# A four-layer gated transformer on one core: second ternary rows rounded on ScalarE, ternary weights on VectorE, instruction lists given by a table

## The reference

```python
x = x + tanh(g_xattn[0]) * _L0_xattn_ref(ctx, ctx, _layernorm(x), ...)
x = x + tanh(g_ffn[0])   * _L0_ffn_ref(_layernorm(x), ...)        # butterfly, folded to two dense products
x = x + tanh(g_xattn[1]) * _L1_xattn_ref(_layernorm(x), ctx, ctx, mask, ...)
x = x + tanh(g_ffn[1])   * _L1_ffn_ref(_layernorm(x), ...)        # top-2 of 8 small experts
x = x + tanh(g_xattn[2]) * _L2_xattn_ref(_layernorm(x), ctx, ctx, ...)
x = x + tanh(g_ffn[2])   * _L2_ffn_ref(_layernorm(x), ...)        # ternary weights
x = x + tanh(g_xattn[3]) * _L3_xattn_ref(_layernorm(x), ctx, ctx, ..., mask)
x = x + tanh(g_ffn[3])   * _L3_ffn_ref(_layernorm(x), ...)        # top-2 of 8 gated experts
```

```python
def bitlinear(x, w, b):
    xn = x * rsqrt(mean(square(x)) + 1e-6)
    xq = clip(round(xn * s), -128, 127) / s        # s = 127 / max(max|xn|, 1e-5), per token
    wq = clip(round(w * t), -1, 1) / t             # t = 1 / max(mean|w|, 1e-5), of the whole matrix
    return einsum('bsi,oi->bso', xq, wq) + b
h = gelu(bitlinear(x, w1, b1))                     # 256 -> 1024
return bitlinear(h, w2, b2)                        # 1024 -> 256
```

## Time and profile before

| | us |
|---|---|
| median of 3 runs | 2720.06 (2715.66 to 2722.37) |
| the profiled execution | 2716.3 |
| its span, first to last instruction | 2714.5 |
| mean granted TensorE clock | 0.975 of full speed |

### The profile page before, as it was taken

How to read it: one execution, slowest core, us unless ns; L and a number is a source line. 1 busy time by engine, 2 the same in 40 slices (tenths; PEclk the granted TensorE clock), 3 DMA queues, 4 the chain that set the end, 5 groups by cost and what they waited for, 6 DMA issues and landing times.

```text
span 2714.5 us, 53760 instructions
## 1 busy us (share of the span) xinstructions
PE 2508.9 (92%) x21317; PEld 1693.2 (62%) x21317; DVE 1688.8 (62%) x4598; ACT 1041.0 (38%) x1654; POOL 976.1 (36%) x2413
## 2 busy tenths in 40 slices
PE   6999788999999988899999998889999998889999
PEld 4566444677767644577776754457776765446776
DVE  6545888755533588955543478885554358887542
ACT  4544345432234445523224444542322444453221
POOL 2352522444332332243442243233444323224342
PEclk8999889999999999999999999999999999899999
DMA  3200100000000000000000000000000000000000
GB/s 125 81 11 1 52 32 14 1 9 9 9 9 12 12 2 14 1 1 9 9 9 9 11 12 1 12 1 9 9 9 9 11 1 12 1 1 1 5 5 8
DMA packets 16280, 37.38 MB, mean 14 GB/s; under 512 B 1408, under 2 KB 11424, under 8 KB 15008
## 3 DMA queue, kind: packets, MB, share of 16 engines
q1 hardware_dynamic: 16032, 33.94, 3.5%
HBM read 29.74 MB, written 4.19 MB: 13 GB/s over the span
## 4 chain that ended last, share of the span: by engine, by line
PE 69%; DVE 22%; ACT 4%; issue 3%; POOL 2%; DMA 0%; SPq 0%; DVEq 0%; ACTq 0%; POOLq 0%
PE P L1322 8%; PE P L1134 4%; PE P L1142 4%; PE P L1181 4%; PE P L1355 4%; PE P L1323 4%; PE P L1193 4%; PE P L1340 4%; PE P L1114 4%; PE P L1331 4%; PE P L1035 4%; DVE mx L1721 4%; PE P L1206 3%; PE P L1031 2%; PE P L1044 1%
## 5 line engine op out<-in xcount | busy, mean ns | idle before, releaser
L1721 DVE TENSOR_REDUCE mx<-P 128x8 f32<-128x1232 f32 x256 | 369.0, 1441 | 178.1 <-PE P L1040 85.9
L1322 PE MATMUL P<-xT,w 128*128 128x256 f32 x1024 | 264.8, 381 | 0.7 <-DVE R L1956 0.3
L1477 ACT ACTIVATE ET<-P 128x2048 f32<-128x2048 f32 x96 | 180.2, 1877 | 162.4 <-PE P L1117 115.3
L1772 DVE SCALAR_TENSOR_TENSOR x<-P,w_first,x 128x512 f32<-128x512 f32 x96 | 73.9, 769 | 252.8 <-PE P L1181 87.0
L1322 PEld LDWEIGHTS P<-xT,w 128*128 128x128 f32 x1024 | 192.0, 190 | 60.7 <-issue 34.9
L792 POOL TENSOR_TENSOR sm<-sm 128x2 f32<-128x2 f32 x384 | 76.0, 198 | 421.0 <-DVE sm L1717 401.0
L1949 DVE SCALAR_TENSOR_TENSOR gu<-gu,P 128x256 f32<-128x256 f32 x128 | 53.9, 421 | 256.7 <-ACT gu L1528 256.7
L1035 PE MATMUL P<-KB,R 32*128 32x308 f32 x1536 | 162.0, 492 | 34.5 <-ACT ET L1477 14.7
L1528 ACT ACTIVATE gu<-P 128x256 f32<-128x256 f32 x128 | 49.2, 384 | 355.9 <-PE P L1323 334.4
L1114 PE MATMUL P<-R,KB 32*128 32x256 f32 x2048 | 169.6, 417 | 14.9 <-DVE mx L1721 14.8
L1434 ACT ACTIVATE xn<-x,sm 128x256 f32<-128x256 f32 x256 | 139.1, 592 | 100.9 <-POOL sm L800 100.9
(11 more groups left out here) (307 smaller groups left out, 5580.8 us busy)
## 6 DMA issues: line engine op xcount, KB each, us to landing
kvw<-in_wkv SPq DMA_DIRECT2D x12, 672.0 KB, 3.9
x<-in_x SPq DMA_DIRECT2D x16, 256.0 KB, 2.8
out<-x SPq DMA_DIRECT2D x16, 256.0 KB, 2.1
w<-in_w SPq DMA_DIRECT2D x2, 1024.0 KB, 5.9
w<-in_wexp SPq DMA_DIRECT2D x1, 1028.0 KB, 7.6
w_w<-in_wcon SPq DMA_DIRECT2D x1, 1024.0 KB, 9.9
w_w<-in_m3t SPq DMA_DIRECT2D x1, 1024.0 KB, 8.3
w<-in_w1q SPq DMA_DIRECT2D x1, 1024.0 KB, 10.3
```

What stands on the lines that cost most here:

```text
L1322: e.matmul(o, wm[:, c, js], s.xT[:, c, :], start=n == c == 0, stop=False, skip_group_check=True)
L1477: e.activation(ET[:].rearrange("p g c -> p (g c)"), quad.rearrange("p g c -> p (g c)"), ACT.Exp, bias=mb1[:, b:b + 1] if l == 1 else 0.0). ...
L1721: e.tensor_reduce(s.mx[:, i, :, 2 * u:2 * u + 2], quad[:, :, 0:2 * NK].rearrange("p g (a k) -> p g a k", a=2), AX.X, ALU.max).then_inc(q_d, 1)
```

## The change

It has five parts.

1. **Rounding.** A new stage `rd` on ScalarE does what L1910 and L1912 did on DVE, in two instructions over 128x1024, with the rounding constant and its negative as biases from a new tile `mg`. The stages of a stream now go `rd` 0, `q2` 0, then `rd` 1 beside `w2` 0, then `q2` 1, `w2` 1. DVE has no part in `q2` any more, and its `gelu2` ends with `d_a`, for which ScalarE's `rd` waits.
2. **Root.** In `gelu2` the root's three rounds are made of `tensor_scalar` instructions over 128x1, one for each half, each waiting for all but the one just ahead of it. Twelve of them take the place of nine over 128x2.
3. **Ternary weights.** The three steps over 128x2048 go from GpSimd to DVE, inside DVE's `tern`.
4. **Lists.** The costs in `parts` are partly new. The rule that picks the next piece is replaced by a table `TURN`: for each engine a string of stream numbers. Of each stream's pieces the order stays; which stream is next on an engine stands in the string.
5. **Fills.** They may now stand before the folding is done too. There are 311 in all, 43 of them ahead of the last folding stages in the list, where there was none.

```diff
-                i, p = min(can, key=lambda c: (start(c[1]) + BACK[c[1][2]].get(c[1][1], 0) + 130.0 * count[c[0]] + 34.0 * c[0],
-                                               count[c[0]] + 0.3 * c[0]))
+                i, p = min((c for c in can if TURN[c[1][2]][taken[c[1][2]]] == str(c[0])), key=lambda c: start(c[1]))
+                taken[p[2]] += 1
...
-                if p[2] == "PE" and at - free["PE"] > 900.0 and done.get("folded") and let["bank"]:
+                if p[2] == "PE" and at - free["PE"] > 900.0 and let["bank"]:
...
                         yield "gelu2", s
-                        for i in range(2):
-                            yield "q2", s, i
-                            yield "w2", s, i
+                        yield "rd", s, 0
+                        yield "q2", s, 0
+                        yield "name", "t"
+                        yield "rd", s, 1
+                        yield "name", "r"
+                        yield "need", "t"
+                        yield "w2", s, 0
+                        yield "name", "w"
+                        yield "need", "r", "w"
+                        yield "q2", s, 1
+                        yield "w2", s, 1
...
+            def rd(s, i):
+                if i == 0:
+                    e.wait_ge(g_const, 13)
+                    e.wait_ge(s.d_a, C.up(s.d_a))
+                e.activation(s.h[:, i, :], s.h[:, i, :], ACT.Identity, bias=mg[:, 0:1],
+                             scale=s.sm[:, 8, i:i + 1]).then_inc(s.a_m, 1)
+                e.wait_ge(s.a_m, C.up(s.a_m))
+                e.activation(s.qt, s.h[:, i, :], ACT.Identity, bias=mg[:, 1:2]).then_inc(s.a_m, 1)
+                C.up(s.a_m)
...
             def tern(c, k):
...
+                e.tensor_scalar(raw, raw, wsc[:, 4 + c:5 + c], MAGIC, ALU.mult, ALU.add).then_inc(d_own, 1)
+                e.wait_ge(d_own, C.up(d_own))
+                e.tensor_scalar(raw, raw, -MAGIC, 1.0, ALU.add, ALU.min).then_inc(d_own, 1)
+                e.wait_ge(d_own, C.up(d_own))
+                e.tensor_scalar(to[:].rearrange("p a b -> p (a b)"), raw, -1.0, None, ALU.max).then_inc(d_quant, 1)
...
             def gelu2(s):
...
+                for n in range(3):
+                    for i in range(2):
+                        own(e.tensor_scalar(a[:, i:i + 1], y[:, i:i + 1], y[:, i:i + 1], hv[:, i:i + 1], ALU.mult, ALU.mult), 1)
+                    for i in range(2):
+                        own(e.tensor_scalar(y[:, i:i + 1], a[:, i:i + 1], 1.5, y[:, i:i + 1], ALU.add, ALU.mult), 1)
...
-            def q2(s, i):
-                e.tensor_scalar(s.h[:, i, :], s.h[:, i, :], s.sm[:, 8, i:i + 1], MAGIC, ALU.mult, ALU.add).then_inc(d_own, 1)
-                e.wait_ge(d_own, C.up(d_own))
-                e.tensor_scalar(s.qt, s.h[:, i, :], -MAGIC, None, ALU.add).then_inc(s.d_p, 1)
```

More of the change, by code:

```diff
@@ L271, in parts @@
             seq = {"near": "PA" if name == "near" and of[1] % 2 else "PD", "grow": "PD", "wide": "AD", "masks": "D", "gb": "D",
-                   "tsum": "DP", "tern": "DG", "raw": "S", "late": "S", "kvw": "s", "store": "S",
-                   "key": "PA" if name == "key" and of[1:] == [0, 0] else "PAG" if name == "key" and of[1] < 2
-                   else "PAg" if name == "key" else "PA", "val": "PDA" if name == "val" and of[1] == 0 else "PD", "norm": "DGA", "bias": "g",
+                   "tsum": "DP", "tern": "D", "raw": "S", "late": "S", "kvw": "s", "store": "S",
+                   "key": "PA" if name == "key" and of[1:] == [0, 0] else "PAG" if name == "key"
+                   else "PA", "val": "PDA" if name == "val" and of[1] == 0 else "PD", "norm": "DGA", "bias": "g",
                    "no": "dg", "pv": "PA" if l == 0 else "P",
-                   "gate1": "PDA", "gate3": "PDA", "q1": "DPA", "gelu2": "AD", "q2": "DPA", "mw": "GPA", "hw": "G"}
+                   "gate1": "PDA", "gate3": "PDA", "q1": "DPA", "gelu2": "AD", "q2": "PA", "rd": "A", "mw": "GPA", "hw": "G"}
             usual = [k for k, t in (("P", pe), ("A", act), ("D", dve)) if name in t]
@@ L326, in late @@
                 return [("near", of[0], of[1] - 2)]
+            if engine == "POOL" and name == "no" and of[2] == 0:
+                return [("values", of[3])]
             if name == "hw" and of[1] == 6:
@@ L354, in early @@
                 return name, *of
+            if engine == "ACT" and name == "pv":
+                return "values", of[3]
             if engine == "DVE" and name in ("h1", "h2"):
@@ L402, in turns @@
                                 yield "after", ("attention", s_.i, 4 * b + l - 2)
+                        yield "name", "free"
                         yield "key", b, l, 0
@@ L405, in turns @@
                             yield "key", b, l, 1
+                        yield "name", "key"
+                        yield "need", "free"
                         yield "val", b, l
+                        yield "name", "val"
+                        yield "need", "key", "val"
                         yield "kvw", b, l
@@ L566, in step @@
             def step(i):
-                while i in live and len(queue[i]) < 24:
+                while i in live and len(queue[i]) < 64:
                     if now[i] is None:
@@ L609, in also @@
                 return [p[7].get(m) for m in late(p[1], p[6], p[2])]
-            table = [1]
+            table, taken = [1], dict.fromkeys(HOP, 0)
             def start(p):
@@ L851, in hw @@
                 C.up(s.g_p)
-            stages = {"key": key, "norm": norm, "bias": bias, "no": no, "mw": mw, "hw": hw, "tern": tern}
+            stages = {"key": key, "norm": norm, "bias": bias, "no": no, "mw": mw, "hw": hw}
             for name, *of in ORDER["POOL"]:
@@ L1887, in gelu2, with own @@
             def gelu2(s):
-                f, sq, ss, am2 = s.sm[:, 8, 0:2], s.sm[:, 9, 0:2], s.sm[:, 10, 0:2], s.sm[:, 11, 0:2]
-                r2, ms = s.sm[:, 3, 0:2], s.sm[:, 4, 0:2]
+                hv, a, y, f, sq, ss, am2 = (s.sm[:, n, 0:2] for n in (0, 1, 3, 8, 9, 10, 11))
+                def own(t, of):
+                    t.then_inc(d_own, 1)
+                    e.wait_ge(d_own, C.up(d_own) - of)
                 e.wait_ge(s.a_d, C.up(s.a_d))
                 e.tensor_reduce(am2, s.h, AX.X, ALU.max, apply_absolute_value=True).then_inc(d_own, 1)
+                C.up(d_own)
@@ new lines, in gelu2 @@
+                own(e.tensor_scalar(a.bitcast(i32), hv.bitcast(i32), 1, None, ALU.logical_shift_right), 0)
+                own(e.tensor_scalar(hv, hv, -0.5, None, ALU.mult), 1)
+                own(e.tensor_scalar(y.bitcast(i32), a.bitcast(i32), -1.0, 1597463007.0, ALU.mult, ALU.add), 0)
+                for n in range(3):
[3 more added lines that the diff above has]
+                        own(e.tensor_scalar(y[:, i:i + 1], a[:, i:i + 1], 1.5, y[:, i:i + 1], ALU.add, ALU.mult), 1)
@@ new lines, in gelu2 @@
+                for i in range(2):
+                    own(e.tensor_scalar(am2[:, i:i + 1], am2[:, i:i + 1], y[:, i:i + 1], 1e-5, ALU.mult, ALU.max), 1 - i)
+                own(e.reciprocal(f, am2), 0)
+                own(e.tensor_scalar(sq, am2, wsc[:, 7:8], None, ALU.mult), 1)
+                for i in range(2):
+                    t = e.tensor_scalar(f[:, i:i + 1], f[:, i:i + 1], 127.0, y[:, i:i + 1], ALU.mult, ALU.mult)
+                t.then_inc(s.d_a, 1)
+                C.up(s.d_a)
```

148 lines of the change are left out of this document (81 added, 67 removed).

## The result

The changed kernel takes **2657.8 us** (median of 4 runs, 2653.3 to 2660.1) where the kernel before takes 2719.7 on the same chip: ratio **0.9774** (0.9757 to 0.9791), 62 us less. In a second session, as `after_again`, it was 0.9761 (0.9744 to 0.9777). The forecast was 2682. The direction was right, the gain was 1.6 times as large, and most of what follows is about its parts, which were further off than their sum.

The account below looks back on a forecast made before the run. TensorE, busy 2508.9 of 2714.5 us, was taken to set the time, with DVE the busier engine in four mixed stretches. Terms -25.7 + 8 - 7 - 2 - 11.4 + 4 = -34.1 us from 2716.3 gave 2682, range 2640 to 2716.

Parts of the forecast that it names:

- Start, 0: First 66 us: 18 fills at the head of TensorE's list change nothing, 0 us (bounds -6 and +5).
- Lists, -11.4: All engines' lists: 45 fewer fills behind the folding mean fewer holes, -11.4 us (bounds +20 and -25).
- Rounding off DVE, -25.7: Four mixed stretches: removing L1910 and L1912 from DVE saves their share on the chain, -25.7 us (bounds -46.6 and 0).
- on ScalarE, +8: ScalarE's queue: rounding pairs of 2.34 us there partly show, +8 us (bounds 0 and 32).
- Ternary weights, -7: Two ternary matrices: GpSimd's steps no longer stop DVE, less DVE's new steps, net -7 us (bounds -11.8 and 0).
- Root, -2: DVE's root: twelve 128x1 steps replace nine that are partly stopped, -2 us (bounds -10.2 and +8).
- a root that is stopped more often: Rival, DVE's root: each of twelve steps stopped like L1688, +14 us for -2, 2698 us; chance 0.05.
- Table loads, +4: ScalarE: 28 more table loads at 1.28 us, mostly hidden as ScalarE is idle, +4 us (bounds 0 and 36).
- Clock, 0: TensorE's granted clock: narrower holes in mixed stretches change nothing net, 0 us (bounds -10 and +10).
- all of DVE's time counts: Rival, four mixed stretches: all DVE time saved counts, each part at its better bound, -91.2 us, 2625 us; chance 0.15.
- ScalarE takes DVE's place: Rival, ScalarE's queue in the four mixed stretches: rounding there holds TensorE up, kernel slower, 2738 us; chance 0.10.
- The lists don't fit the chip: Rival, all lists: their gain of 11.4 us turns into +20, 2714 us, no change; chance 0.10.

Follow-up runs that it names:

- experiment 5: Changed kernel with the rounding alone put back on DVE in the old sequence, other pieces and fills in the new order: 2697.5 us, ratio 0.9923 to the kernel before.
- experiment 8: Changed kernel, ScalarE still rounding, plus six unused DVE steps at each of the two places per stream where the rounding stood: 2723.1 us, ratio 1.0019.
- experiment 3: Kernel before with rounding on ScalarE, ternary weights on DVE and new root, but every engine's old order and old fill places: 2716.3 us, ratio 0.9999.
- Experiment 1: Changed kernel without the 43 fills ahead of the folding's end, all else alike: 2651.5 us, ratio 0.9750 to the kernel before.
- experiment 2: Changed kernel's lists and start fills, but rounding back on DVE, ternary weights back on GpSimd and the old root: 2724.8 us, ratio 1.0027.
- experiment 9: Old order with the three edits (rounding on ScalarE, ternary weights on DVE, new root), plus unused DVE steps where the rounding stood: 2722.1 us, ratio 1.0015.

## Why the prediction was right and wrong, by its steps

The sum said -34 us; measured were -56 between the profiled executions and -62 by the ratio. The direction held for one of the two reasons given, DVE's load in the mixed stretches (experiments 5 and 8). The other, TensorE's wait at the transposes, was not what paid: it keeps its size in experiment 3. That the sum came as near as it did is partly luck. By the runs the edits are worth 73 us in the new order for 26.7 in the sum, and the lists with the start cost 7 where the sum had a gain of 11.4: two errors that work against each other. These steps failed:

- **Start, 0: about -18 us by the traces**, far outside its bounds (-6 and +5); no run takes the start's order alone. I costed the 18 fills at the head and not the order behind them. Experiment 1 shows that it is the order: 216 more matmuls in 66 us without one start fill, with 5.6 us less idle time and a clock of 0.97. The 23.3 us of idle time in the earlier trace rows were named, and a start in which TensorE stands idle and at a clock of 0.81 should have had a term with both.
- **Lists, -11.4 as a gain of their own: alone they cost 7 us** (experiment 2), the start's 18 included. The bound of +20 held it. The step that failed is behind the number: the sum treats lists and edits as separate terms that add. They don't here: edits alone 0, lists alone +7, and both together -62 (-65 in the second session). A list is right for one set of costs. I used the count of fills as evidence of the lists' worth, but it is a plan's own view of its holes, and a plan made with the new costs.
- **Rounding off DVE, -25.7, and on ScalarE, +8.** Together -17.7. In the old order it is worth nothing together with the other two edits (experiment 3), in the new one 44 us (experiment 5). The reading from the chain was that of a kernel whose TensorE list put the transposes right behind the root, so it found each first half there, and would have found it on whichever engine rounded: TensorE's wait stayed 39 us. What the new order is worth with less DVE work can't be read from that chain. My bound of -46.6, all of DVE's time, was nearly met. Of ScalarE's side the sizes were right (pair 2.38 for 2.34 us, busy 1145.6 for 1152), and the wait for it was 11.5 us, within 0 to 32.
- **Ternary weights, -7: 20 us in the new order**, outside the bounds. I priced the stop by the idle time that TensorE shows beside it in the old order, 4.4 us, which is what that list happened to cover. DVE's own steps I had at 4.3 us a matrix, and they take 3.75. The stop itself was read rightly: with the steps back on GpSimd, a DVE instruction of 7.08 us is back. (So the Trainium skill's rule, SBUF — State Buffer, section Who interferes with whom, that the holder of the shared ports blocks the other for its whole instruction, fits these runs as well.)
- **Root, -2: 9 us in the new order**, just within the bound of -10.2. I took 163 ns for each of twelve steps; they take 266 and 207, stopped or not (the shortest L1964 is 261 ns). But the two halves overlap (0.46 us for a pair of the 266 ns ones), and a round takes 0.62 us (368.12 to 368.74) where the old one takes 0.59, while the number of steps around it fell. The rival of a root that is stopped more often is refuted.
- **Table loads, +4.** There is no run on them, so this stays open. The Gelu still starts 0.02 us behind one.
- **Clock, 0.** The mean clock rose from 0.975 to 0.981, and TensorE's own work became 19 us shorter. Part of that is the start (0.81 to 1.00 in 66 us), part the narrower holes: the last two mixed stretches are at 0.99 and 0.98 where they were at 0.95 and 0.94, while the first two gain 0.01 each. The bounds of -10 and +10 were too narrow. It is a consequence of the other terms, and it should have stood in the sum as a share of each of them: here a third of what is gained (19 of 56 us).

What should show it: the four stretches are 5 to 11 us shorter (6 to 15 in the repeat, and I had 5 to 10), the wait for the rounding is 11.5 us and for ScalarE, no long DVE instruction is left, ScalarE's time is right, and the full stretches keep their length. DVE's busy time fell by 44 us in all, not 50: the ternary steps add 7.5, and the root takes 37.5 us in L1964 and L1966 for 33.6 in the three old groups.

Of the rivals, *all of DVE's time counts* describes the new order (44 us for 44 in experiment 5, 66 to 70 for 57 in experiment 8), though the time of 2625 also took the lists' better bound. *ScalarE takes DVE's place* shows in experiment 3, where TensorE waits for it just as long as for DVE's rounding. *The lists don't fit the chip* is true of the lists alone.

**What stays open:** why the old order, with the rounding on ScalarE, has 60 us of room on DVE at these places and the new one none, and what each edit does alone in the old order. It isn't how full DVE is: in the four mixed stretches it is busy for 759 of 902 us in experiment 9 and 741 in experiment 8.

## What to carry to other kernels

In a kernel whose engines work through fixed lists, an edit that spares an engine time can show nothing until the lists are made again for it, and new lists can show nothing without the edit, as here: test both together before dropping either, and don't add their terms. Whether an engine's time counts can be measured in one run with steps that nobody reads, put at the place in question, for the kernel as it then stands; here its busy share was 82% in the order where they cost 70 us and 84% in the order where they cost 4. And look at the start of a kernel for itself, at the idle time and the granted clock: some 18 of the 56 us between the two traces were there.

## What the runs showed of the hardware that was not expected

- The same unused work on DVE, some 60 us, cost 70 us in one order and 4 in another.
- A `tensor_scalar` over a single column takes longer with pointer operands: 128x1 with two of them 266 ns (never under 261) and with one 207, where 128x2 steps of two tensors take 161 to 163 and a 128x2 `tensor_scalar` with constants alone (L1958, L1960) 167 to 169. Two of the 266 ns ones that don't wait for each other overlap, 0.46 us for both.
- DVE's steps over 128x2048 take 1.23 to 1.29 us; GpSimd's take 2.0, 5.4 and 7.1, and the small DVE step beside the longest of them takes 7.08 us.
- What fills are worth differs with the place: 8 us from 61 of them at the start of the old order, nothing that shows from 43 in the new one (0.97 without them), 8 to 12 us from all 311, and nothing from denser ones, 466 in all, though these raised the mean clock to 0.988.
